# TensorE's order in the attention loop of layer 0: projection pieces behind the first two maxima products, scores of the second half with the second head first

## The reference

```python
ada = silu(c) @ W_ada + b_ada
shift_msa, scale_msa, gate_msa, shift_mlp, scale_mlp, gate_mlp = split(ada, 6)
x = x + gate_msa * attention(modulate(layernorm(x), shift_msa, scale_msa))
x = x + gate_mlp * mlp(modulate(layernorm(x), shift_mlp, scale_mlp))
...
scores = einsum('blhd,bmhd->bhlm', q * D ** -0.5, k)      # 16 heads of 18 columns
attn = softmax(scores, axis=-1)
o = einsum('bhlm,bmhd->blhd', attn, v)
```

## Time and profile before

| what | value |
|---|---|
| median of 3 runs | 917.32 us (916.29 to 917.46) |
| the profiled execution | 916.52 us |
| its span | 914.4 us |
| PE busy | 792.0 us (87%) |
| DVE busy | 649.9 us (71%) |
| ACT busy | 533.5 us (58%) |
| POOL busy | 269.9 us (30%) |

### The profile page before, as it was taken

How to read it: one execution, slowest core, us unless ns; L and a number is a source line. 1 busy time by engine, 2 the same in 40 slices (tenths; PEclk the granted TensorE clock), 3 DMA queues, 4 the chain that set the end, 5 groups by cost and what they waited for, 6 DMA issues and landing times. The chain is left out here.

```text
span 914.4 us, 16701 instructions
## 1 busy us (share of the span) xinstructions
PE 792.0 (87%) x6096; PEld 365.0 (40%) x6096; DVE 649.9 (71%) x1273; ACT 533.5 (58%) x751; POOL 269.9 (30%) x347
## 2 busy tenths in 40 slices
PE   1568989999988989898878899999979875999996
PEld 0334222222222222222215465566646553666564
DVE  4849788888888898989707856646687798844521
ACT  4433576777676777767885636536547634546630
POOL 4320110214463411010005426341223456421122
PEclk9979799999999999999999899999989996999999
DMA  7202000110112110000040011011676720000000
GB/s 227 69 21 72 20 27 27 28 47 20 40 34 59 34 34 14 22 19 20 2 108 0 11 40 41 1 38 44 156 177 163 173 52 16 12 8 27 26 27 27
DMA packets 52127, 45.35 MB, mean 50 GB/s; under 512 B 23898, under 2 KB 41236, under 8 KB 52055
## 3 DMA queue, kind: packets, MB, share of 16 engines
q1 hardware_dynamic: 47613, 36.35, 15.3%
q10 hardware_dynamic: 4442, 8.04, 2.8%
HBM read 27.66 MB, written 9.46 MB: 41 GB/s over the span
## 5 line engine op out<-in xcount | busy, mean ns | idle before, releaser
L921 DVE TENSOR_REDUCE row_max<-ps 128x1 f32<-128x512 f32 x512 | 322.3, 683 | 60.3 <-PE ps L1653 59.4
L1413 ACT ACTIVATE probs<-ps 128x1024 f32<-128x1024 f32 x256 | 248.5, 1018 | 53.9 <-PE ps L1680 53.2
L1653 PE MATMUL ps<-stack_area 54*128 54x512 f16 x512 | 150.2, 388 | 27.1 <-DVE row_max L921 21.8
L1692 PE MATMUL ps<-probs,mlp_area 128*32 128x512 f32 x1024 | 137.2, 608 | 0.4 <-ACT probs L1413 0.4
L1680 PE MATMUL ps<-stack_area 56*128 56x512 f16 x512 | 110.1, 384 | 9.6 <-ACT probs L1413 9.3
L1653 PEld LDWEIGHTS ps<-stack_area 54*128 54x128 f16 x512 | 37.0, 93 | 191.5 <-DVE row_max L921 175.8
L1782 PE MATMUL ps<-mlp_area,w_fc 128*128 128x512 f16 x504 | 110.8, 379 | 1.7 <-issue 0.9
L1803 PE MATMUL ps<-w_fc,mlp_area 128*128 128x288 f16 x864 | 107.7, 286 | 4.6 <-DVE mlp_area L1061 4.6
L1454 ACT ACTIVATE mlp_area<-ps 128x512 f32<-128x512 f32 x72 | 42.9, 595 | 97.7 <-PE ps L1782 95.4
L1803 PEld LDWEIGHTS ps<-w_fc,mlp_area 128*128 128x128 f16 x864 | 83.8, 98 | 27.3 <-DVE mlp_area L1061 3.9
L738 POOL TENSOR_SCALAR neg_scaled<-neg_max 128x16 f32<-128x16 f32 x16 | 4.1, 254 | 292.8 <-DVE neg_max L928 292.8
(11 more groups left out here) (163 smaller groups left out, 1108.7 us busy)
## 6 DMA issues: line engine op xcount, KB each, us to landing
stack_area<-tokens SPq DMA_DIRECT2D x124, 36.0 KB
qkv_rows<-part_area ACTq DMA_DIRECT2D x14, 252.0 KB
qkv_rows<-probs ACTq DMA_DIRECT2D x10, 252.0 KB
x_sb<-in_x SPq DMA_DIRECT2D x4, 576.0 KB, 7.3
w_raw<-in_L_cond_W_fc SPq DMA_DIRECT2D x4, 576.0 KB
tokens<-qkv_rows SPq DMA_DIRECT2D x64, 36.0 KB
v_sb<-qkv_rows SPq DMA_DIRECT2D x16, 144.0 KB
w_raw<-in_L_cond_fc_w SPq DMA_DIRECT2D x4, 576.0 KB
```

Of the source, the lines that this page charges most:

```text
L921: nc.vector.reduce_max(row_max[:, p % 2, t, j, half:half + 1], bank(bk), AX.X).then_inc(max_done, 1)
L1413: nc.scalar.activation(probs[:, n % 2, 2 * c:2 * c + 2, :].rearrange("p h n -> p (h n)"), ps[:, 2 + 2 * c:4 + 2 * c, :].rearrange("p b n - ...
L1653: nc.tensor.matmul(bank(bk), stacks[rows, p % RING, 0, t * P:(t + 1) * P], stacks[rows, p % RING, 1, half * 512:(half + 1) * 512], start=T ...
L1692: mm = nc.tensor.matmul(bank(6)[at:at + VW, :], v_pad[:, TB * (p // BPAIR) + n, 2 * (p % BPAIR) + j, :], probs[:, n % 2, 2 * c + j, :], st ...
```

## The change

Three tables now give the order in a slot. The projection's seven pieces are cut into 2, 1, 2 and 2, of which the last three follow each other directly, so that a P slot is: W, two pieces, S0, S1, O, five pieces, A, S2, B, S3. In slots without a projection step the kinds of steps stand as before. `SCORE_HEADS` makes B's two products in the order head 1, head 0, with `scores_ready` raised by the product of head 0; A's stay head 0, head 1. `plan_banks()` reads the same table; the banks and the users before them come out as before.

```diff
+        PE_ORDER = ['W', 'P0', 'S0', 'S1', 'O', 'P1', 'P2', 'P3', 'A', 'S2', 'B', 'S3']
+        PART_RANGES = [(0, 2), (2, 3), (3, 5), (5, 7)]
+        SCORE_HEADS = [(0, 1), (1, 0)]
...
-                for j in range(2):
+                for j in SCORE_HEADS[c]:
                     rows = slice(HROWS * j, HROWS * j + SR)
                     mm = nc.tensor.matmul(bank(2 + 2 * c + j), stacks[rows, p % RING, 1, n * P:(n + 1) * P],
...
-                    if s > 0:
-                        weigh(*divmod(s - 1, SLOTS))
-                    project(part, 0, 2)
-                    side(maxima[0:1])
-                    project(part, 2, 4)
-                    side(maxima[1:2])
-                    project(part, 4, 6)
-                    side(other_of(s))
-                    project(part, 6, 7)
...
+                    later = SCORES_FIRST <= s < NPAIR * SLOTS - 1
+                    for step in PE_ORDER:
+                        if step == "W" and s > 0:
+                            weigh(*divmod(s - 1, SLOTS))
+                        if step[0] == "P":
+                            project(part, *PART_RANGES[int(step[1])])
+                        if step[0] == "S":
+                            side(maxima[int(step[1]):int(step[1]) + 1])
+                        if step == "O":
+                            side(other_of(s))
+                        if step in "AB" and later:
+                            scores(*divmod(s + 1, SLOTS), "AB".index(step))
```

More of the change, by code:

```diff
@@ L433, in plan_banks @@
                 maxima, others = maxima_of(s), other_of(s)
-                for i, step in enumerate(part_of(s) + maxima[:2] + others + maxima[2:]):
+                order = [x for k in PE_ORDER for x in (part_of(s) if k == 'P0' else maxima[int(k[1]):int(k[1]) + 1] if k[0] == 'S' else others if k == 'O' else [])]
+                for i, step in enumerate(order):
                     now = s + i / 6
```

## The result

| | median us | runs | ratio to before, 95% interval |
|---|---|---|---|
| before | 916.81 (915.94 to 917.46) | 4 | |
| changed | 910.15 (909.47 to 910.30) | 4 | 0.9925 (0.9909 to 0.9941) |
| changed, a second comparison | 909.89 (907.29 to 911.37) | 6 | 0.9909 (0.9893 to 0.9925) |
| changed, a third comparison | 908.82 (907.96 to 911.58) | 4 | 0.9903 (0.9887 to 0.9920) |

The change makes the kernel 0.75 to 1.0% faster. The forecast was 910.1 us. The kernel before beside the second comparison has 17 executions (median 916.47 us), of which one took 971.34 us at a granted clock of 0.841 and is left out of the ratios. The profiled execution of the changed kernel has a span of 907.9 us against 914.4, 6.5 us less.

The account below looks back on a forecast made before the run. P slots were taken as bound by PE's own work. 7.2 (P slots) - 0.48 (pair 9's wait) + 0.5 (early slots) = 7.2 us off the 917.32 us median: 910.1 us, range 908.0 to 912.3 (0.79), 907.3 to 913.3 for 8 in 10.

Parts of the forecast that it names:

- P slots are PE-bound, 0.48 us each: 15 attention-loop slots with projection pieces: PE's own work bounds them, S0 to A falls from 2.00 to 1.52 us, 7.2 us together.
- The rival of a slower run of five: P slots: pieces start 0.27 us apart throughout, so 0.30 us saved a slot and 912.8 us; chance 0.06.
- S1's bank fits: P slots: DVE frees S1's bank 0.16 us before S1's new start at 343.79, beside S0.
- Pair 9 gives one back: First maxima product of pair 9: PE comes 0.48 us earlier and waits 0.48 us longer for its stacks, minus 0.48 us.
- Slots -12 and 0: The two early slots given a new order: 0.58 us saved in the first, about 0.5 in the second at the lower clock.
- The clock's return costs up to 0.55 us: Near 100 us: the clock may return at the same time, so 1.1 us more work runs at half speed.
- the early part: Slots -12 and 0 together: 1.08 us saved, less the full cost of the clock's return, taken as 0.5 us.
- The exchange of heads costs and brings nothing: B's products in all 127 slots: PE already takes head 1 beside S2 and head 0 beside S3, so 0 us.
- The rival that rested on it: Strict program order: the exchange of heads saves 0.22 us where PE bounds the slot, 3.5 us more, 906.6 us; chance 0.05.
- the slower one: B's written order head 1, head 0 breaks pairing, 0.22 us a slot where not hidden; 923.3 us at 60 slots; chance 0.04.

Follow-up runs that it names:

- experiment 3: The changed kernel with all seven projection pieces ahead of S0 and S1: 919.4 us, ratio to before 1.003.
- experiments 1 and 2: First: the kernel before with only B's heads exchanged, 917.83 us; second: the changed kernel with B's heads in the old order, 908.19 us.
- experiment 4: The changed kernel with both of B's products reading head 0's rows of the stacks: 915.65 us, ratio to before 0.9982.
- experiment 2: The changed kernel with B's products in the old order, head 0 then head 1: 908.19 us, ratio to before 0.9914.

## Why the prediction was right, and where it was not

- *P slots are PE-bound, 0.48 us each.* Right: 0.46 and 0.43 us. The slots behind kept their lengths, as the bank times had said. The term was 7.2 us and measured 6.8. S0 to A came out at 1.55 us against 1.52, and the four narrower slots, which had been taken like the others, save 0.43. The rival of a slower run of five is out: the five pieces start 0.27 and then 0.21 to 0.22 us apart, 1.29 us to the last end.
- *S1's bank fits.* Right, S0 and S1 start together, and experiment 3 shows the edge from the other side.
- *Pair 9 gives one back.* Right: the wait went from 1.17 to 1.64 us, slot 60 from 3.70 to 4.18.
- *Slots -12 and 0.* 0.58 us forecast and 0.60 measured (3.74 to 3.14); 0.45 to 0.5 forecast and 0.60 measured for S0 to A in slot 0 (3.59 to 2.99).
- *The clock's return costs up to 0.55 us.* This step failed. I took it that the clock would come back at the same time as before and charge half of the time won. It fell and came back some 3 us sooner, at another place of the work, and gave 0.97 us in slot 1. The rows of before were one execution's: two other traces with the old order in these slots had slot 1 at 2.49 us.
- *What was not in the sum:* the lower clock in slot 61, 1.06 us. I had seen the wait grow and priced it as waiting alone.
- *That 910.1 met 910.15 is luck.* By the account of slots the early part gave 2.1 us (0.60, 0.75 and 0.97, less 0.20) and not 0.5, the P slots gave 0.4 less than forecast, the clock in slot 61 took 1.06, and 0.9 are spread ahead of the loop and behind it. So the trace is 6.4 us shorter and not 7.2, and the rest is the median of the kernel before, 916.81 in the comparison and 917.32 in the forecast. The sum of the P slots is what was understood.
- *The exchange of heads costs and brings nothing.* Right, by experiments 1 and 2, and for the reason given: PE pairs by head already. (There are 128 such slots, not 127: the trace has 512 score products.) By its trace experiment 4 shows more of it: PE also takes S3 ahead of two B products. The Trainium skill ("TensorE: Matmul & The Clock Gate", section The mechanism) has matmuls in strict program order. This kernel's traces and times say otherwise for products in different rows of the array (two steps and a P slot of 4.33 us in either order of B's heads, where a third step costs 0.22 us), and the measurement decides. The rival that rested on it is out, and so is the slower one: B's products pair as well when head 1 is written first.

## What to carry to other kernels

Two engines that hand banks to each other can both look nearly full while single slots belong to one of them; find those slots by laying the starts side by side, and change only what stands in them. A run of equal products is worth having only as far as the partner engine still gets its input in time: the order with the fewest changes of height was 11.2 us slower than experiment 2 on the same chip. And where a saved half microsecond ends in a wait for a transfer, that wait grows by as much (1.17 to 1.64 us here) and may bring the lower clock with it, so it is the next thing to remove.

## What the runs showed of the hardware that was not expected

- PE starts matmuls out of program order where their rows of the array are free: with S2, B, B, S3 in the program and both B in S2's rows, S3 started with S2 (343.91), ahead of both. Two such pairs in place of three steps are worth 0.22 us a slot where PE bounds it, 7.5 us over the kernel against experiment 2 on the same chip. Their semaphores still rise in program order (344.74 for the last B product, 344.77 for S3).
- TensorE's lower clock isn't fixed by the kernel: of six traces with the same wait of 1.6 us three had it behind that wait, for 1.1 us of extra time each. With that, executions of the same kernel differ by a microsecond.
